# An audio tower on one core: attention computed by pairs of heads, with the softmax division moved behind the second matmul

## The reference

```python
h = _L0_tok_ref(x, ...)                       # 16 x 375 x 128
h = h + _L0_attn_ref(_layernorm(h), gamma, beta, wq1, wqd, ...)
h = h + _L0_ffn_ref(_layernorm(h), ...)
# attention: 8 heads of 64, layer norm again inside, then
#   y = w1 @ xn; y = wd0*y[:-2] + wd1*y[1:-1] + wd2*y[2:]   (three taps, for q, k and v)
sim = q @ k.T + bias * slope                  # bias = -|i - j|, causal mask
attn = softmax(sim)
out = concat_heads(attn @ v) @ wout.T
```

## Time and profile before

| | us |
|---|---|
| median of 3 runs (1565.75 to 1567.41) | 1566.08 |
| the profiled execution | 1568.55 |
| its span in the profile | 1566.8 |
| TensorE busy in the span | 1354.8 |
| VectorE busy | 952.7 |
| ScalarE busy | 671.4 |
| GpSimd busy | 264.4 |

### The profile page before, as it was taken

The page is one execution under the profiler, slowest core; times in us unless marked ns, Lnnn a source line. Parts: engine busy times, 40 slices in busy tenths (PEclk is TensorE's granted clock), DMA queues, the critical chain, the costliest instruction groups (busy, mean ns, idle before and its releaser), DMA issues. The chain is left out here.

```text
span 1566.8 us, 26688 instructions
## 1 busy us (share of the span) xinstructions
PE 1354.8 (86%) x7905; PEld 1089.1 (70%) x7905; DVE 952.7 (61%) x3107; ACT 671.4 (43%) x1759; POOL 264.4 (17%) x262
## 2 busy tenths in 40 slices
PE   6999999999369999989999899999997896466663
PEld 5999999999356777766767667677665685355553
DVE  3433434334569898879878798788874566621211
ACT  2334334333235655656546565456653341021211
POOL 6000000000010001001110000100000400178885
PEclk9999999999679999999999999999998898687877
DMA  4000000000100000000000000000000112044542
GB/s 106 17 15 20 20 10 20 20 10 20 35 11 10 2 22 23 22 21 17 10 17 21 21 20 10 14 21 12 12 12 20 28 34 60 6 79 81 97 82 39
DMA packets 93851, 43.86 MB, mean 28 GB/s; under 512 B 31295, under 2 KB 90088, under 8 KB 93752
## 3 DMA queue, kind: packets, MB, share of 16 engines
q1 hardware_dynamic: 69960, 36.25, 8.5%
q0 software_dynamic: 23808, 6.69, 3.3%
HBM read 29.52 MB, written 10.18 MB: 25 GB/s over the span
## 5 line engine op out<-in xcount | busy, mean ns | idle before, releaser
L783 ACT ACTIVATE P<-P,nmax 125x375 f32<-125x375 f32 (+2 forms) x384 | 189.1, 494 | 292.1 <-DVE nmax L923 291.9
L287 PE MATMUL bank<-h1hl,W2hl 128*128 128x376 f32 x1536 | 278.0, 336 | 2.9 <-DVE h1hl L402 2.9
L287 PEld LDWEIGHTS bank<-h1hl,W2hl 128*128 128x128 f32 x1536 | 264.0, 189 | 3.1 <-DVE h1hl L402 3.1
L624 PE MATMUL bank<-QK 64*125 64x375 f32 (+2 forms) x768 | 197.8, 391 | 13.4 <-DVE nmax L923 13.4
L624 PEld LDWEIGHTS bank<-QK 64*125 64x125 f32 x768 | 112.8, 185 | 75.8 <-DVE nmax L923 25.0
L364 ACT ACTIVATE h<-bank,b2c 128x375 f32<-128x375 f32 x128 | 73.5, 574 | 207.3 <-PE bank L287 207.3
L923 DVE CUSTOM_DVE_ANT_0 P<-bank,nbias 125x375 f32<-125x375 f32 (+2 forms) x384 | 139.7, 413 | 2.6 <-PE bank L624 2.5
L1569 ACT ACTIVATE hE<-bank,EB 128x375 f32<-128x375 f32 x64 | 36.7, 573 | 199.0 <-PE bank L1544 196.4
L680 PE MATMUL bank<-WVT,xnThl 128*125 128x512 f32 x432 | 115.7, 413 | 3.0 <-DVE QK L972 3.0
L913 DVE TENSOR_SCALAR P<-P,prec 125x375 f32<-125x375 f32 (+2 forms) x384 | 111.9, 347 | 4.5
L865 POOL TENSOR_SCALAR lnve<-lnmv 125x3 f32<-125x3 f32 x32 | 10.1, 315 | 575.6 <-DVE lnmv L891 575.6
(11 more groups left out here) (196 smaller groups left out, 2363.4 us busy)
## 6 DMA issues: line engine op xcount, KB each, us to landing
X<-in_x_dram SPq DMA_DIRECT2D x34, 375.0 KB
EW<-in_L_ffn_w_dram SPq DMA_DIRECT2D x32, 256.0 KB
token_table<-row SPq DMA_DIRECT2D x16, 210.9 KB
tTall<-tT SPq DMA_DIRECT2D x16, 187.5 KB, 2.3
out_dram<-oS SPq DMA_DIRECT2D x16, 187.5 KB
tTall<-in_L_tok_W_dram SPq DMA_DIRECT2D x1, 1024.0 KB, 7.1
EB<-in_L_ffn_b_dram SPq DMA_DIRECT2D x16, 62.5 KB
tok<-token_table,ids POOLq DMA_INDIRECT x48
```

The lines of the kernel that those rows point to most:

```text
L287: last = nc.tensor.matmul(bank[4 + m % 2][:, :NE], W2hl[:, a, k, m * 128:(m + 1) * 128], h1hl[:, p, b, k], start=(k == 0 and n == 0), stop ...
L624: last = nc.tensor.matmul(bS[unit][:PT_, at:at + w], QK[r:r + DH, 0, c, i * PT_:(i + 1) * PT_], QK[r:r + DH, 1, c, :w], start=True, stop=True)
L783: nc.scalar.activation(P[:, h % 4, SEG[q]:SEG[q] + w], P[:, h % 4, SEG[q]:SEG[q] + w], ACT.Exp, bias=nmax[:, h % 4, q:q + 1], scale=-1.0, ...
```

## The change

Attention goes by pairs of heads c = 0 to 3, each in two parts: part 0 (even steps) has the 375-column tile of both heads, part 1 (odd steps) the tiles of 250 and 125 columns of both. Head q of the pair (0 or 1) uses rows 64 q to 64 q + 63 and bank `bS[q]`, and the two heads' matmuls alternate. A part waits until VectorE has read the part before out of the banks.

P is no longer normalised. VectorE takes the reciprocals of a pair's row sums broadcast over 64 columns each (384 elements), TensorE transposes them beside P (three transposes more per pair, `bT[half][:, N:TW]`), ScalarE copies them out with P (up to 500 columns instead of 375), and VectorE multiplies the attended sum in PSUM by them when it takes it to `OT`. The transposes of a pair now come one pair behind its scores and wait for its exponentials, the attend step two pairs behind. ScalarE makes all copies of transposed P, and VectorE those of `OT`. The transposed P block is read 128 wide for 125, into three columns that hold the next block or zeros.

The two layer norms in a row become one, with a variance of var (1 + eps) + eps^2, and GpSimd applies it, as it does the gate's. cellmax goes to GpSimd too, with two buffers. In ScalarE's order the exponentials stand ahead of the first taps and of the copies; the relu of the overlap stands ahead of the copy of V.

```diff
...
-            SEG = (0, N, N + PT_)
-            ORDER = (2, 0, 1)
-            LN = 9
+            SEG = (N, N + PT_, 0)
+            LN = 7
+            PW = 2 * N + 3
+            TW = N + PT_
...
-            P = sb_("P", [PT_, 4, 2 * N])
+            P = sb_("P", [PT_, 4, PW])
             nmax = sb_("nmax", [PT_, 4, NT])
-            psum_ = sb_("psum_", [PT_, 4, NT])
-            prec = sb_("prec", [PT_, 4, NT])
-            PT = sb_("PT", [PT_, 4, 2 * N])
+            psum_ = sb_("psum_", [PT_, 2, NT, 2])
+            prec = sb_("prec", [PT_, 2, NT, 2, DH])
+            PT = sb_("PT", [128, 2, 4, TW])
...
+            def pair_before(b, c, back):
+                return b + (c - back) // 4, (c - back) % 4
+            PARTS = ((2,), (1, 0))
+            ORDER = ((2, 0), (2, 1)), ((1, 0), (0, 0), (1, 1), (0, 1))
...
+                def scores(b, c, part):
+                    n = 4 * b + c
...
+                    wait(pe, s_s, 6 * n + 2 * part)
+                    for i in PARTS[part]:
+                        w, at = (i + 1) * PT_, 0 if i else 2 * PT_
+                        for q in range(2):
+                            r = DH * q
+                            last = nc.tensor.matmul(bS[q][:PT_, at:at + w],
...
+                    last.then_inc(s_sp, 1)
+                def transpose_probs(b, c, q):
+                    n, r = 4 * b + c, c % 2
+                    if q == 0:
+                        pe.wait_ge(s_ex, 6 * n + 6)
+                    for half, blocks in enumerate((((0, 0), (1, 0), (2, 0)), ((1, 1), (2, 1), (2, 2)))):
+                        wait(pe, (s_pt0, s_pt1)[half], 2 * n + q)
+                        for k, (i, j) in enumerate(blocks):
+                            f = SEG[i] + j * PT_
+                            last = nc.tensor.transpose(bT[half][:, k * PT_:(k + 1) * PT_],
+                                                       P[:, 2 * r + q, f:f + 128], ident[:PT_, :PT_])
+                        i = 2 * q + half - 1
+                        if i >= 0:
+                            if i == 0:
+                                pe.wait_ge(s_rc, n + 1)
+                            last = nc.tensor.transpose(bT[half][:, N:TW],
+                                                       prec[:, r, i].rearrange("p q d -> p (q d)"),
+                                                       ident[:PT_, :PT_])
+                        last.then_inc(s_tp, 1)
...
+                    n, r = 4 * b + c, c % 2
+                    pe.wait_ge(s_pt0, 2 * n + 2)
+                    pe.wait_ge(s_pt1, 2 * n + 2)
...
+                    wait(pe, s_o, n)
+                    for j in range(NT):
+                        half, at, w = min(j, 1), (j // 2) * 2 * PT_, N - j * PT_
+                        for q in range(2):
+                            last = nc.tensor.matmul(bO[DH * q:DH * (q + 1), j * PT_:N],
+                                                    V[:, u, j, (2 * c + q) * DH:(2 * c + q + 1) * DH],
+                                                    PT[:PT_, r, 2 * q + half, at:at + w],
+                                                    start=(j == 0), stop=(j == NT - 1))
...
+                            scores(b, c, part)
...
+                        m, d = pair_before(b, c, 1)
+                        if valid(m):
+                            transpose_probs(m, d, part)
+                        m, d = pair_before(b, c, 2)
+                        if part == 0 and valid(m):
+                            attend(m, d, u if c >= 2 else v_)
...
+                            pe.wait_ge(s_lnp, 4 * (m + 1))
...
+                            pe.wait_ge(s_gp, 4 * (m + 1))
...
+                def exps(b, c, part):
+                    n, r = 4 * b + c, c % 2
+                    for k, (i, q) in enumerate(ORDER[part]):
+                        w = (i + 1) * PT_
+                        act.wait_ge(s_s, 6 * n + 2 * part + k + 1)
+                        nc.scalar.activation(P[:, 2 * r + q, SEG[i]:SEG[i] + w], P[:, 2 * r + q, SEG[i]:SEG[i] + w],
+                                             ACT.Exp, bias=nmax[:, 2 * r + q, i:i + 1], scale=-1.0,
+                                             accum_out=psum_[:, r, i, q:q + 1]).then_inc(s_ex, 1)
...
+                def copy_probs(b, c, q):
+                    n, r = 4 * b + c, c % 2
+                    wait(act, s_o, n - 1)
+                    for half, w in enumerate((TW if q else N, TW)):
+                        act.wait_ge(s_tp, 4 * n + 2 * q + half + 1)
+                        nc.scalar.copy(PT[:, r, 2 * q + half, 0:w], bT[half][:, :w]
+                                       ).then_inc((s_pt0, s_pt1)[half], 1)
...
+                            exps(b, c, part)
...
+                            first_tap(m, d, 0)
+                            first_tap(m, d, 1)
+                        m, d = pair_before(b, c, 1)
...
+                            copy_probs(m, d, part)
+                        m, k = (b + 3, h - 3) if h else (b + 2, TT_ - 1)
+                        if h not in (1, 2) and valid(m):
+                            act.wait_ge(s_ov, 6 * m + k + 1)
+                            wait(act, s_ein, m)
+                            nc.scalar.activation(Wt[:, k], overlap[:, k % 2], ACT.Relu).then_inc(s_wt, 1)
...
+                def ln_apply(dst, m, mv, r, s, n):
+                    nc.gpsimd.tensor_tensor(dst[:, :, 0:C], Hall[:, m], mv[:, :, 0:1].broadcast_to([PT_, NT, C]),
+                                            ALU.subtract).then_inc(s, 1)
+                    pool.wait_ge(s, n + 3)
+                    nc.gpsimd.tensor_tensor(dst[:, :, 0:C], dst[:, :, 0:C],
+                                            r[:, :, None].broadcast_to([PT_, NT, C]), ALU.mult).then_inc(s, 1)
...
+                        if h == 1 and valid(b + 2):
+                            m = b + 2
+                            wait_apart(pool, s_lnd, LN * (m + 1), s_on[1])
+                            rsqrt(lnve, lnr, lnmv, 1.0 + EPS, EPS * EPS, s_lnp, 4 * m)
+                            wait(pool, s_xtp, m)
+                            ln_apply(n2, m, lnmv, lnr, s_lnp, 4 * m)
+                        if h >= 2 and valid(b + 3):
+                            m, k = b + 3, h - 2
+                            wait_apart(pool, s_csb, m + 1, s_on[1])
+                            wait_apart(pool, s_ov, 6 * m + k - 1, s_on[1])
+                            nc.gpsimd.tensor_scalar(cellmax[:, k % 2], grid0[:], csb[:, TT_ + k:TT_ + k + 1], None,
+                                                    ALU.max).then_inc(s_cm, 1)
...
+                            wait_apart(pool, s_g, LN * (m + 1), s_on[1])
+                            rsqrt(gve, gr, gmv, 1.0, EPS, s_gp, 4 * m)
...
+                            ln_apply(row, m, gmv, gr, s_gp, 4 * m)
...
+                def biased_max(b, c, part):
+                    n, r = 4 * b + c, c % 2
+                    if part == 0:
+                        wait(dve, s_tp, 4 * (n - 1))
+                    wait_apart(dve, s_sp, 2 * n + part + 1, s_on[0])
+                    for i, q in ORDER[part]:
+                        w, at = (i + 1) * PT_, 0 if i else 2 * PT_
+                        nc.vector.tensor_tensor_reduce(
+                            out=P[:, 2 * r + q, SEG[i]:SEG[i] + w], in0=bS[q][:PT_, at:at + w],
+                            in1=nbias[:, 2 * c + q, (2 - i) * PT_:N], scale=1.0, scalar=MASKED, op0=ALU.add,
+                            op1=ALU.min, accum_out=nmax[:, 2 * r + q, i:i + 1]).then_inc(s_s, 1)
...
-                            nc.vector.reciprocal(prec[:, hh], psum_[:, hh]).then_inc(s_rc, 1)
-                            dve.wait_ge(s_rc, n + 1)
-                            for q, i in enumerate(ORDER):
-                                w = (i + 1) * PT_
-                                nc.vector.tensor_scalar(P[:, hh, SEG[q]:SEG[q] + w], P[:, hh, SEG[q]:SEG[q] + w],
-                                                        prec[:, hh, q:q + 1], None, ALU.mult).then_inc(s_pn, 1)
+                        m, d = pair_before(b, c, 2)
+                        if part == 1 and valid(m):
+                            n = 4 * m + d
+                            dve.wait_ge(s_pv, n + 1)
+                            wait(dve, s_wo, m)
+                            nc.vector.tensor_tensor(OT[:, d].rearrange("p (t i) -> p t i", i=PT_),
+                                                    bO[:, :N].rearrange("p (t i) -> p t i", i=PT_),
+                                                    PT[:, d % 2, 1:4, N:TW], ALU.mult).then_inc(s_o, 1)
...
+                            biased_max(b, c, part)
+                        m, d = pair_before(b, c, 1)
+                        if part == 0 and valid(m):
+                            n = 4 * m + d
+                            dve.wait_ge(s_ex, 6 * n + 6)
+                            nc.vector.reciprocal(prec[:, d % 2], psum_[:, d % 2, :, :, None].broadcast_to(
```

(5 more changed lines are left out.)

204 lines of the change are left out of this document (47 added, 157 removed).

## The result

The changed kernel takes 1663.95 us (median of 4 runs, 1658.63 to 1670.29), the kernel before beside it 1565.91. The ratio is 1.0625, 95% interval 1.0587 to 1.0663. I had forecast 1552, so the sign was wrong; the rival with the slow reciprocal (1670) is what happened. The profiled execution took 1664.34 us, its span is 1662.0.

What follows compares the result with a forecast made beforehand. TensorE bounds; its work falls to 39.2 us a turn, but 5.0 of waits restore 44.2. Turns 0, jumps -22, last batches -3, dips +10: -15 on 1568.6, itself 2.5 above the median, gives 1552 us; own range 1530 to 1582, overall 1520 to 1690.

Steps and rivals of the forecast that it cites:

- the rival with the slow reciprocal: VectorE's 384-element reciprocal costs about 9 ns an element, not one column time: +117 us, 1670; chance 0.29.
- The row halves: Two heads' scores run at once on TensorE: 0.75 us a part instead of 1.46, saving 5.7 us a turn.
- TensorE's work: TensorE's work per turn falls from 43.3 to 39.2 us: scores save 5.7, added transposes cost 1.6.
- (d): TensorE waits about 0.1 us at each of the other three reciprocals in a turn, 0.3 us together.
- break-even of 2.5 ns: Reciprocal price per element, some 2.5 ns, from which the forecast turns to slower.
- (a): TensorE's projection waits for ScalarE's copy of V: 1.8 us at step 6, 0.4 at step 0.
- (b): After the pooling, VectorE's late statistics delay maxima and reciprocal; TensorE waits 1.3 us at the reciprocal's transpose.
- (c): Output projection at step 3 waits 1.2 us for the last pair's OT, made by VectorE behind late taps.
- The jumps: VectorE's shorter loop, 315 instructions for 456, no longer stalls at its 4 jumps: 4 x 5.5 = 22 us go.
- The clock: TensorE's clock dips after waits, 1 to 1.5 us each; one every second turn adds 10 us.
- waits cost twice: A TensorE wait also lowers its granted clock afterwards; such a dip costs 1 to 1.5 us.
- GpSimd at nothing: Work moved onto GpSimd, some 14 us of a 40 us turn at 0.99 us each, costs nothing.

Runs made afterwards that it cites:

- e14: e1 with both heads of a pair taken from rows 0 to 63 in the scores, so their matmuls cannot run at once; 1565.7 us.
- e10: e1 with first taps ahead of exponentials, V's copy ahead of the relu, and the loop written out; 1468.5 us.
- e1: Changed kernel with the reciprocal taken of a pair's 6 row sums, then a VectorE copy spreading it to 384 columns, same place; 1523.7 us.
- e2: Changed kernel with the same 384-element reciprocal moved to the end of VectorE's odd step; 1600.2 us.
- e13: e1 with VectorE's loop body one turn instead of two, 167 instructions and nine jumps; 1510.0 us.
- e6: e1 with the attention's loop of five passes written out on all engines; 1497.8 us.

## Why the prediction was wrong

**The row halves: right.** I took 0.75 us for a part by the attend row; it is 0.83 to 0.84. e14 shows that serial they take 1.45.

**TensorE's work: right to half a microsecond.** I had 39.2 us a turn. e10, which hardly waits, is busy 39.70 us and its turn is 40.33.

**The reciprocal: the step that failed.** The sum took "one element per column time" for (d), 0.55 us, and 0.1 us of wait. It takes 2.55 us. The rows that I had, 168 ns for three elements and 150 for one, give 9 ns each by their difference and were read as fixed cost by the minimum of 142. The line through 187 and 448 ns says both: a fixed 150 ns and 6.25 ns an element. At three elements the two cannot be told apart, and I gave the cheaper reading the larger chance (0.38 for the forecast, 0.29 for this rival), though it was the value on which the sign hung. My chances taken together had slower at 0.57: the forecast named the likeliest single case, not the likelier sign. My break-even of 2.5 ns an element was passed by far. The rival's size (1670 for 1664) was right partly by luck: by its rule, 2.0 us more for each of four waits, less what (a) takes back, 6.25 ns would give 1552 plus some 70 to 80; the jumps that stayed (+22) and the clock make up the rest to 1664.

**(a) V late at step 6.** Forecast 1.8 us; 0.5 in after, where the reciprocal's waits cover it, 0.84 in e1, 2.0 in e2. Right in kind; in e1, the kernel that the sum describes, mis-sized by a factor of two.

**(b) behind the pooling.** Forecast 1.3 us at prec; it is 2.0 in after at 673.95, little more than at the other pairs. What I had not listed is a wait ahead of it: the k projection needs the bank of the gate's transposed probabilities, which VectorE copies to `pTs` behind the statistics, 0.7 to 1.2 us. In e1 the two together are 1.2 us (0.8 for `pTs`, 0.4 for prec, 676 to 690 us).

**(c) the output projection for OT.** Forecast 1.2; none in after, up to 0.5 in e1, 1.7 in e2.

**The jumps: wrong.** -22 us was taken since 456 instructions became 315. VectorE's stretch of 3.89 us is 4.6 now; the bound was between 167 and 315 instructions, and I had only ScalarE's 249 as a row below it. The kind was right (e13), the number not. The value of a jump, 5.5 us, was close to the 6.5 of e6; in after itself a turn with a jump is only 3.2 us longer than one without.

**The clock: mis-sized.** I took a dip every second turn, +10 us. In after the clock of a loop turn is 0.90, and it costs the difference of 44.64 and 40.06 us, 4.6 us a turn, about 60 in all. With the short reciprocal it is 1.00 outside the jumps. My sentence "waits cost twice" holds for the reciprocal's waits, whose 5.5 extra us a turn brought 4.6 of clock, but not as a rule: in e2 7.5 us of waits in a turn brought none.

**GpSimd at nothing: right for the turns.** cellmax takes 1.25 us, more than the 0.99 taken, and the tensor_tensors 0.83, less; between 606 and 1060 us neither TensorE nor VectorE waits for GpSimd. Where the stage starts, before 500 us, they do: VectorE 10.4 us for cellmax in 13 waits, TensorE once 4.6 us for the applied norm, where it had waited up to 7.9 for VectorE's before.

**The rest of the structure was better than forecast.** e1 is the changed kernel as I had imagined it, with a cheap reciprocal. Without the 22 us of jumps my sum makes 1574; it takes 1524. Of the 50 us, 14 turns of 42.9 instead of 44.2 make 18; 13 are loop turns, which I had taken from 44.2 although they took 45.5 before; 10 are the clock dips that did not come; the first turns before the first output projection are 8 shorter (from the last group L343 at 407.13 in before and 405.23 in e1 to 525.66 and 515.49). That last term is loose: e6, with the same program ahead of its loop, has only 3 of the 8.

## What to carry to other kernels

A step moved from few elements to many needs its price per element, and two short rows of it never give that; where the sign hangs on it, forecast the time at both prices and look where it stands in the order. Divide once and spread by a copy. An order on one engine is worth nothing while something longer covers it, so remove the longest wait first and try the orders again. A TensorE wait of some 2 us that recurs can cost nearly double, as in after, or only itself, as in e2: read the granted clock behind it.

## What the runs showed of the hardware

- VectorE's fp32 reciprocal: 187, 448, 1348 and 2549 ns for 6, 48, 192 and 384 elements a partition, 6.25 ns each; a copy over the same 384 takes 0.36 us in the median and 0.52 in the mean (e1).
- Scores of two heads (four matmuls of 375 columns, fp32) in the two halves of the rows, each into its own bank: 0.83 us for what takes 1.45 one after the other.
- VectorE's jump: 4.0 to 4.6 us idle with listings of 315 and 323 instructions (after, e1), 2.2 to 2.5 where a 2.54 us instruction stands last before it (e2), none with 167 (e13), nor on ScalarE with 249.
- TensorE's clock: behind a wait of 2.0 us it was 0.50 over the next 5.7 us; with waits of 1.3 to 2.0 us at every pair it was 0.90 over a turn (after), with waits of 0.4 to 0.8 us 1.00 (e1), and 1.00 also in e2's turns with 7.5 us of waits, up to 2.0 us long. In one turn of after it fell behind the waits of 1.88 us (at 768.04) and 2.04 us (783.26), where the attend group took 2.39 and 2.77 us, and stayed up behind those of 1.86 us (745.98) and 1.31 us (756.72), where it took 1.49.
